# One sum for four groups of edges: the edge network's segment sums at register offsets in one PSUM bank

## The reference

```python
src, dst = (edge_index[0], edge_index[1])
edge_input = jnp.concatenate([x[src], edge_attr], axis=-1)
messages = _gelu(edge_input @ mW1 + mb1) @ mW2 + mb2
gates = jax.nn.sigmoid(_gelu(edge_input @ gW1 + gb1) @ gW2 + gb2)
aggregated = jax.ops.segment_sum(messages * gates, dst, num_segments=x.shape[0])
combined = jnp.concatenate([x, aggregated], axis=-1)
update = _gelu(combined @ uW1 + ub1) @ uW2 + ub2
h = x + update
```

## Time and profile before

| | us |
|---|---|
| median of 3 runs | 10,818.27 |
| lowest, highest | 10,817.15, 10,834.14 |
| the profiled execution | 10,833.28 |
| its span, first to last instruction | 10,831.3 |
| granted TensorE clock, mean over the span | 0.84 |

### The profile page before, as it was taken

How to read it: one execution, slowest core, us unless ns; L and a number is a source line. 1 busy time by engine, 2 the same in 40 slices (tenths; PEclk the granted TensorE clock), 3 DMA queues, 4 the chain that set the end, 5 groups by cost and what they waited for, 6 DMA issues and landing times. The chain is left out here.

```text
span 10831.3 us, 151063 instructions
## 1 busy us (share of the span) xinstructions
PE 8115.2 (75%) x42144; PEld 5216.6 (48%) x42144; DVE 4910.5 (45%) x11836; ACT 2686.7 (25%) x6600; POOL 6404.8 (59%) x6424
## 2 busy tenths in 40 slices
PE   4777777777777777777777577787777578877876
PEld 3555555555555555555554333343334333333333
DVE  7666666666666666666666122222222122222222
ACT  3444444444444444444443000000000000000000
POOL 4555555555555555555555666666664666666664
PEclk7888888888888888888887788888887688888887
DMA  4444444444444444444444466666665466665656
GB/s 148 128 137 137 134 140 132 139 132 139 132 138 135 136 138 133 139 132 139 131 139 152 144 212 215 207 228 209 211 214 200 157 208 223 216 220 200 222 207 213
DMA packets 936184, 1818.04 MB, mean 168 GB/s; under 512 B 280495, under 2 KB 748736, under 8 KB 878448
## 3 DMA queue, kind: packets, MB, share of 16 engines
q10 hardware_dynamic: 65600, 773.65, 18.9%
q1 hardware_dynamic: 618592, 578.41, 16.9%
q0 software_dynamic: 251856, 464.10, 16.1%
HBM read 1361.12 MB, written 454.48 MB: 168 GB/s over the span
## 5 line engine op out<-in xcount | busy, mean ns | idle before, releaser
L956 POOL DMA_INDIRECT hid<-src_table,src_ids x3127 | 3121.3, 998 | 2450.0 <-ACT msg L1352 1514.8
L1234 PE MATMUL bd<-ring,table_sb 128*96 128x480 f32 x6272 | 2898.5, 610 | 382.7 <-issue 381.5
L1234 PEld LDWEIGHTS bd<-ring,table_sb 128*96 128x96 f32 x6272 | 1070.0, 175 | 1954.7 <-issue 1954.7
L1001 POOL DMA_INDIRECT hid<-conv_table,hid x1596 | 1552.2, 973 | 715.1 <-issue 488.4
L1149 PE MATMUL sg<-hot,msg 128*98 128x64 f32 x6272 | 817.2, 283 | 1256.1 <-ACT msg L1352 1256.1
L1149 PEld LDWEIGHTS sg<-hot,msg 128*98 128x98 f32 x6272 | 733.3, 196 | 1379.3 <-issue 1303.6
L1001 POOL DMA_INDIRECT feat_in<-conv_table,hid x1056 | 1022.6, 968 | 588.6 <-issue 342.8
L1126 PE MATMUL bd<-one_hot_dst,one_hot_src 128*128 128x168 bf16 (+1 forms) x10368 | 1246.2, 275 | 88.5 <-issue 87.6
L1966 DVE TENSOR_TENSOR acc<-acc,sg 96x64 f32 x400 | 87.3, 218 | 2365.6 <-remote 1368.1
L1361 ACT ACTIVATE blocks<-bd 128x480 f32<-128x480 f32 (+1 forms) x1152 | 657.8, 571 | 1971.7 <-PE bd L1126 941.6
L1126 PEld LDWEIGHTS bd<-one_hot_dst,one_hot_src 128*128 128x128 bf16 x10368 | 1013.5, 110 | 108.6 <-issue 94.3
(11 more groups left out here) (248 smaller groups left out, 10323.9 us busy)
## 6 DMA issues: line engine op xcount, KB each, us to landing
ring<-adjacency ACTq DMA_DIRECT2D x448, 1680.0 KB
adjacency<-blocks SPq DMA_DIRECT2D x384, 980.0 KB
attr<-in_attr SPq DMA_DIRECT2D x392, 128.0 KB
hid<-src_table,src_ids POOLq DMA_INDIRECT x3127
hid<-conv_table,hid POOLq DMA_INDIRECT x1596
feat_in<-conv_table,hid POOLq DMA_INDIRECT x1056
conv_table<-table_sb SPq DMA_DIRECT2D x28, 336.0 KB, 2.5
feat_half<-feat_keep SPq DMA_DIRECT2D x56, 168.0 KB
```

The costliest lines, as they stand in the source:

```text
L956: pool.indirect_dma_start(out=hid[s][:, t, :], out_offset=None, in_=src_rows, in_offset=bass.IndirectOffsetOnAxis(ap=src_ids[s // 2][:, j: ...
L1001: pool.indirect_dma_start(out=conv_g[j][slot][:, t, :], out_offset=None, in_=conv_rows[l], in_offset=bass.IndirectOffsetOnAxis(ap=conv_ids ...
L1234: op = nc.tensor.matmul(side_ps[w].rearrange("r (o z) -> r o z", o=UNIT_OCTETS), table_sb[:, D * k:D * (k + 1)], ring[slot][:, :, OCTET_FA ...
```

## The change

The two windows of an iteration become one span of 160 columns that holds the four groups of two iterations. In the setup DVE takes the smallest first node of each four groups as the span's base, bounds each group's offset from it to 96, and lowers the group's own first node by what is over. In the loop PE loads the two offsets of an iteration into registers and writes each group's sums at its offset in `sg[0]`, over what stands there. A matmul of zeros over the 160 columns opens each span. DVE adds the whole span once, in slot 0 of every second iteration, behind `add`; the wait of PE for it stands before quad 0 of every second iteration. The counts on `s_acc` change with that on POOL and ACT too. The four preparing iterations are written out instead of looped.

```diff
@@ -49,14 +49,19 @@
-ACC = NODES + WINDOW
+SPAN_ITERS = 2
+SPANS = ITERS // SPAN_ITERS
+SPAN_GROUPS = GROUPS // SPANS
+LAST_OFFSET = 96
+SPAN = LAST_OFFSET + WINDOW
+ACC = N + SPAN
...
-SETUP_STEPS = 21
+SETUP_STEPS = 28
...
@@ -366,7 +375,7 @@
-        sums = [sg[0][:, WINDOW * g:WINDOW * (g + 1)] for g in range(GROUPS_PER_ITER)]
+        sums = sg[0][0:ACC_ROWS, 0:SPAN]
...
@@ -597,14 +607,13 @@
-                prepare(0, None)
-                with eng.Fori(1, SLICES - 1) as c:
-                    prepare(c, None)
-                prepare(SLICES - 1, (0, o0))
+                for c in range(SLICES):
+                    prepare(c, (0, o0) if c == SLICES - 1 else None)
...
@@ -1100,6 +1109,12 @@
+            def load_offsets(it):
+                _, offsets = nc.values_load_multi_w_load_instructions(
+                    offset_i[0:1, bass.ds(it * GROUPS_PER_ITER, GROUPS_PER_ITER)], engines=[mybir.EngineType.PE],
+                    min_val=0, max_val=LAST_OFFSET, skip_runtime_bounds_check_because="DVE has bounded them")
+                return offsets
...
@@ -1128,7 +1143,8 @@
-            def edges(it, n, first, last, build, ahead):
+            def edges(it, n, first, last, build, ahead, half, span):
+                offset = load_offsets(it)
...
@@ -1143,18 +1159,20 @@
                     pe.wait_ge(s_gated, QUADS_PER_ITER * n + s + 1)
-                    if s % 2 == 0 and not (first and s == 0):
-                        pe.wait_ge(s_acc, GROUPS_PER_ITER * n + s // 2)
+                    if half == 0 and s == 0:
+                        if not first:
+                            pe.wait_ge(s_acc, span)
+                        nc.tensor.matmul(sums, zero[:, :].to_broadcast([P, ACC_ROWS]), first_base[:, 0:SPAN], start=True, stop=False)
                     for t in range(QUAD):
-                        op = nc.tensor.matmul(sums[s // 2][0:ACC_ROWS, :], msg[s % 2][:, t, :],
-                                              hot[s % 2][:, t, :], start=(s % 2 == 0 and t == 0),
-                                              stop=(s % 2 == 1 and t == QUAD - 1))
+                        op = nc.tensor.matmul(sg[0][0:ACC_ROWS, bass.ds(offset[s // 2], WINDOW)], msg[s % 2][:, t, :],
+                                              hot[s % 2][:, t, :], start=False,
+                                              stop=(half == SPAN_ITERS - 1 and s == QUADS_PER_ITER - 1 and t == QUAD - 1))
                     op.then_inc(s_seg, 1)
...
@@ -1579,7 +1597,23 @@
-            do.did(v.tensor_scalar(top[:, 1:2], top[:, 0:1], 0.0, None, ALU.max))
+            do.did(v.tensor_reduce(span_base[:, :], first_base[:, :].rearrange("p (s g) -> p s g", g=SPAN_GROUPS),
+                                   AX.X, ALU.min))
+            do.wait()
...
+            do.did(v.tensor_scalar(offset_i[:, :], base_f[0:1, :], float(LAST_OFFSET), None, ALU.min))
...
@@ -1705,10 +1730,15 @@
-            def window_sum(it, n, g, first):
-                add_window(it, n, g, ACC_ROWS, first, s_seg, QUADS_PER_ITER * n + 2 * g + 2, s_acc)
-
-            def edges(it, n, first, last, build, ahead):
+            def span_sum(it, n, span):
+
+                start = dve.value_load(span_i[0:1, bass.ds(it // SPAN_ITERS, 1)], min_val=0, max_val=N)
+                total = acc[0:ACC_ROWS, bass.ds(start, SPAN)]
+                after(dve, s_acc, span)
+                dve.wait_ge(s_seg, QUADS_PER_ITER * (n + SPAN_ITERS))
+                v.tensor_tensor(total, total, sums, ALU.add).then_inc(s_acc, 1)
+
+            def edges(it, n, first, last, build, ahead, half, span):
...
@@ -1717,10 +1747,6 @@
                     gate(it, n, s, not (first and s < 2))
-                    if s == 0 and not first:
-                        window_sum(it - 1, n - 1, 1, False)
-                    if s == 2:
-                        window_sum(it, n, 0, first)
                     if s < 2 and build:
                         spread_sides(1, 2 * s, build[1])
...
@@ -1733,11 +1759,19 @@
                         add(it + 1, n + 1, s + 2 - QUADS_PER_ITER)
+                    if s == 0 and half == 0 and not first:
+                        span_sum(it - SPAN_ITERS, n - SPAN_ITERS, span - 1)
                 if last:
-                    window_sum(it, n, 1, False)
+                    span_sum(it - (SPAN_ITERS - 1), n - (SPAN_ITERS - 1), span)
```

More of the change, by code:

```diff
@@ L584, in edge_pass @@
                 w0 = eng.snap(r * OCTET_PAIRS)
+                s0 = eng.snap(r * SPANS)
                 def prepare(c, ahead):
@@ L589, in prepare @@
                         part(c, done)
-                    iteration(c, n0 + c, isinstance(c, int) and c == 0, False, None, ahead)
+                    iteration(c, n0 + c, c == 0, False, None, ahead, c % SPAN_ITERS, s0 + c // SPAN_ITERS)
                     if end:
@@ L946, in _, with gather @@
                 pool.wait_ge(s_table_out[p], 16 * (CHUNKS // 2))
-            def gather(it, n, first, last, build, ahead):
+            def gather(it, n, first, last, build, ahead, half, span):
                 for s in range(QUADS_PER_ITER):
@@ L1580, in _ @@
             do.wait()
-            do.did(v.tensor_scalar(top[:, 1:2], top[:, 0:1], 0.0, None, ALU.max))
+            do.did(v.tensor_reduce(span_base[:, :], first_base[:, :].rearrange("p (s g) -> p s g", g=SPAN_GROUPS),
+                                   AX.X, ALU.min))
+            do.wait()
+            by_span = span_base[:, :].unsqueeze(2).to_broadcast([P, SPANS, SPAN_GROUPS])
+            in_spans = [t.rearrange("p (s g) -> p s g", g=SPAN_GROUPS) for t in (base_f[:, :], first_base[:, :])]
+            do.did(v.tensor_tensor(in_spans[0], in_spans[1], by_span, ALU.subtract))
+            do.wait()
+            do.did(v.tensor_scalar(offset_i[:, :], base_f[0:1, :], float(LAST_OFFSET), None, ALU.min))
+            do.wait()
+            do.did(v.tensor_scalar(base_f[:, :], base_f[:, :], -float(LAST_OFFSET), 0.0, ALU.add, ALU.max))
+            do.wait()
+            do.did(v.tensor_reduce(top[:, 1:2], base_f[:, PAD_TILES // GROUP:], AX.X, ALU.max))
+            do.did(v.tensor_tensor(first_base[:, :], first_base[:, :], base_f[:, :], ALU.subtract))
+            do.wait()
+            do.did(v.tensor_tensor(top[:, 0:1], top[:, 0:1], top[:, 1:2], ALU.add))
+            do.wait()
+            do.did(v.tensor_scalar(top[:, 1:2], top[:, 0:1], 0.0, float(N), ALU.max, ALU.min))
             do.wait()
@@ L1597, in _ @@
             new_source(CHUNKS - 1, (CHUNKS - 1) % 2)
-            def add_window(it, n, g, rows, first, s_sum, value, s_done):
-                start = dve.value_load(base_i[0:1, bass.ds(it * GROUPS_PER_ITER + g, 1)], min_val=0, max_val=NODES)
-                window = acc[0:rows, bass.ds(start, WINDOW)]
-                if not first:
-                    dve.wait_ge(s_done, GROUPS_PER_ITER * n + g)
-                dve.wait_ge(s_sum, value)
-                v.tensor_tensor(window, window, sums[g][0:rows, :], ALU.add).then_inc(s_done, 1)
             def place_windows(do, slots, shift, flag):
@@ L1735, in edges @@
                         add(it + 1, n + 1, s + 2 - QUADS_PER_ITER)
+                    if s == 0 and half == 0 and not first:
+                        span_sum(it - SPAN_ITERS, n - SPAN_ITERS, span - 1)
                 if last:
-                    window_sum(it, n, 1, False)
+                    span_sum(it - (SPAN_ITERS - 1), n - (SPAN_ITERS - 1), span)
             def edges_start(r):
-                place_windows(Steps(dve, s_shift, r * 3), iota, pass_f[:, bass.ds(r, 1)], None)
+                do = Steps(dve, s_shift, r * 5)
+                shift = pass_f[:, bass.ds(r, 1)]
+                place_windows(do, iota, shift, None)
+                do.did(v.tensor_scalar(span_now[:, :], span_base[0:1, :], shift[0:1, :], float(N), ALU.add, ALU.min))
+                do.wait()
+                do.did(v.tensor_copy(span_i[:, :], span_now[:, :]))
+                do.wait()
                 wait_apart(dve, s_round[0], r + 1)
```

13 lines of the change are left out of this document (9 added, 4 removed).

## The result

| | us |
|---|---|
| kernel before, median of 8 runs beside the changed kernel | 10,823.5 |
| changed kernel, median of 8 runs (10,846.4 to 10,872.1) | 10,854.4 |
| ratio, 95% interval | 1.0027, 1.0017 to 1.0038 |
| forecast | 11,080 |

The change costs 31 us; 257 were forecast (263 with the setup, against the profiled execution). The profiled execution of the changed kernel has a span of 10,851.0 us against 10,831.3, 19.7 us more.

What follows compares the result with a forecast made beforehand. Bound: the beat of gathers and TensorE's late signals, not TensorE's work. Profiled 10,833.3 + 259 (late quad) + 4 (setup) = 11,096 us, forecast 11,080 because that execution ran 15 us above the median; range 10,710 to 11,160.

Steps and rivals of the forecast that it cites:

- What bounds the kernel: Edge-network beat of about 14.05 us: 2.4 to the first gather, 10.1 of gathers, 1.45 behind; TensorE's work not the bound.
- Removed sums and loads: 392 VectorE window sums and their register loads, 294 not replaced: worth nothing; 90 us gain if VectorE were on the path.
- frees nothing: Taking the window-sum wait from VectorE gains nothing in these beats, since it waits for the same late TensorE signals.
- rival (c): VectorE is on the path: 90 us less, 10,728 us; chance 0.06.
- The sum, the zero matmul, TensorE's lateness: Span sum 0.32 us behind add, zero matmul 0.31 to 0.55; TensorE 2.8 to 3.4 us late once in two iterations.
- GpSimd's lateness: Second four gathers start 1.3 to 3.4 us late, 2.7 taken; 96 spans, 259 us, bounds 125 and 326.
- lower clock behind the longer gaps: TensorE's clock is lower after longer idle before the quad; reason for taking 2.7 us, nearer the upper end.
- Rival (a): GpSimd's stop between its fours frees TensorE's late signals; beat about 1 us shorter, 96 us, 10,725 us; chance 0.18.
- (b): Both cancel: some spans as forecast, some as rival (a); within 0.2%, about 10,820 us; chance 0.12.
- Rival (d): TensorE is the bound: late start paid in full, 298 us, plus register loads 77 us, 11,197 us; chance 0.08.
- Setup: Seven more small VectorE steps ahead of the loop, about 4 us on the path.

Runs made afterwards that it cites:

- h1: Kernel before with TensorE's attribute products done twice into the same place, on a holding chip: 10,935.5 us, 1.0002.
- e1: Kernel before with its window sums, their register loads and the waits for them left out, on a prompt chip: 8,896.0 us, 1.0045.
- e6: Kernel before plus TensorE's two register loads at the head of each iteration, values unused, on a prompt chip: 8,858.2 us, 0.9998.
- e4c: Changed kernel with the one sum right behind VectorE's first gate step, on a holding chip: 10,782.5 us, 0.9959 to the kernel before.
- e8: Kernel before with three GpSimd fills between first and second four of eight gathers, every second iteration, on a holding chip: 10,999.4 us, 1.0049.
- e2: Kernel before without the block matmuls of each quad's last tile, a quarter of them, on a prompt chip: 8,856.8 us, 0.9997.

## Why the prediction was wrong, point by point

**What bounds the kernel: right for this sort of chip.** The beat is the gathers and what follows them. Doubling TensorE's attribute products changed nothing (h1), and the copy comes behind the last gather. On a prompt chip the same program is bound by GpSimd alone, and the forecast couldn't know that there are such chips.

**Removed sums and loads: right on prompt chips** (e1, e6). On the holding chip "frees nothing" looks too strong: with the sum early the change is 48 us faster than before (e4c), which would be about half of rival (c)'s 90; by what way is argued.

**The sum, the zero matmul, TensorE's lateness: right.** The sum takes 0.32 us, the quad starts 0.48 us behind the zero matmul. On the chip of the result the zero matmul starts 3.1 to 3.6 us behind the end of the weighing, where the quads of the kernel before that follow a pause start 0.14 us behind it in the middle: 3.0 to 3.4 us late, with 2.8 to 3.4 forecast. TensorE waits 3.9 us a span (180.3 us, 46 times) on the prompt chip, 4.0 us on the chip of the result (200.4 us, 50 times in 70 spans).

**GpSimd's lateness: the stop is right, its price wrong. This is the step that failed.** The prediction put 2.7 us of stop and multiplied by 96, 259 us, with the rest of the beat as it was. The stop is there, 3.6 us on average in the late beat and 2.7 to 3.0 in the three that should have had none, but the signals that TensorE had finished come out in it and the pause behind the eighth gather shrinks from 3.9 to between 0.6 and 1.6 us. The beats stay at 14.0 to 14.4 us. The late quad costs 74 us (e4c against the result, two chips), 0.8 us a span. On a prompt chip there is nothing held to give back and it costs 92 us, 1.0 us a span; there the quad is simply less late for GpSimd than I had worked out, 0 in a third of the spans and 1.3 us in the middle. Why the stop spread to all four beats stays open.

Two readings in the working were off without harm to the sum. By its own 1.3 to 3.4 us the late beat was to be 15.4 to 17.5 us, not 16 to 17.5. And the lower clock behind the longer gaps isn't in the rows: rows 4 and 9 have the quad at 0.90 us behind 2.14 us of idle time and at 1.58 behind 1.61. The whole trace bears the statement out: a record of L1149 takes 250 ns on average where its quad stood behind less than 1 us of idle time, and 374 ns behind 4 us or more.

**Rival (a) was the mechanism, and (b) came nearest.** (a) had the rule that decides, but not the size or the sign: it said 96 us faster, and the late quad costs. (b) said no change within 0.2%; measured are 0.27%. (a) was weighed down by "they turn late at the same place of TensorE's program whatever the clock". That observation was true and proved nothing: the place in the program and the place among the gathers were the same in all rows I had, because the kernel was regular. Only a kernel in which they part, such as e8 or the changed one, tells them apart. The +31 us of the result can then be split into some 74 us of late quad less some 44 us (0.41%) that the rest of the change gains, the setup and the source phase included. This is one difference split by one more run on another chip, not two measurements.

**Rival (d)** fell with h1 on this sort of chip, and with e2 on a prompt one.

**Setup: right**, 4 us; the further 12 us in the source phase weren't foreseen and stay unexplained.

**What stays open.** What makes a chip hold TensorE's signals, and by what way gathers do it; how long a stop must be; and why the idle time of GpSimd comes out nearly the same in a thousand us of the kernels before and changed. No version here beats the kernel before on both sorts of chip: the early sum is 0.4% faster on the holding and 1.3% slower on the prompt ones, the stop in every eight gathers is 1.35% faster on the holding ones and wasn't run on the prompt ones, where shorter or rarer stops cost 2%.

## What to carry to other kernels

A delay on an engine that already pauses is not worth its length times its count: find what ends the pause, and ask whether the delay brings that forward. When two explanations place an event at the same point of a regular trace, neither may be priced until something parts them. And a small change can differ in sign from chip to chip (the early sum: 0.4% faster, 1.3% slower): where the time of the same kernel differs by a fifth, numbers from one chip's trace don't hold for the other.

## What the runs showed of the hardware

- The same program took 8,857 to 8,863 us on three chips and 10,831 to 10,957 us on three others. On the slower sort TensorE's signals rise late behind the recorded ends of their matmuls while GpSimd issues indirect DMAs (block parts 0.7 us in the middle, a tenth over 2.5, up to some 6), and of 962 that came over 1 us late 835 rose while no gathers ran; on the faster sort all rise after 0.01 us.
- A fill of GpSimd doesn't hold these signals as its gathers do: 2.4 us of fills in every eight gathers made the kernel 1.35% faster.
- An indirect DMA of 64 rows takes GpSimd 0.90 us, one of 128 rows 0.95 us, with 0.30 us to the next.
- On a prompt chip gathers take 0.96 us on average with no VectorE instruction of two SBUF inputs beside them, and 1.13 to 1.26 us beside 0.5 us or more of such; the one shown took 2.19.
